# Layer norm, attention and a mixture of experts on one core: experts by chunk, a regrouping done by DMA, and crossed score matmuls

## The reference, cut to what matters

```python
def attn(x, Wq, Wk, Wv):               # x is the layer norm of the input, 4 x 1024 x 256
    Q = (x @ Wq.T).reshape(H, b, s, dkh)          # H = 16 heads, dkh = 16
    K = (x @ Wk.T).reshape(H, b, s, dkh)
    V = (x @ Wv.T).reshape(H, b, s, dvh)
    scores = jnp.einsum('hbqd,hbkd->hbqk', Q, K)
    atten = jax.nn.softmax(scores, axis=-1)
    out = jnp.einsum('hbqk,hbkd->hbqd', atten, V).reshape(b, s, -1)
    y = out + x
    ...                                           # normalised over tokens and features of a batch
def ffn(x, w_gate, w_in, w_out):       # E = 8 experts, two of them weighted per token
    ...
    for e in range(E):
        h = xt @ w_in[e].T
        y = y + gates[:, e:e + 1] * (h @ w_out[e].T)
x = x + attn(xn, ...) + ffn(xn, ...)
```

## Time and profile before

| | us |
|---|---|
| median of 3 runs (lowest to highest) | 1100.63 (1099.38 to 1101.2) |
| the execution that was profiled | 1102.04 |
| its span (first to last instruction) | 1100.2 |

### The profile page before, as it was taken

How to read it: one execution, slowest core, us unless ns; L and a number is a source line. 1 busy time by engine, 2 the same in 40 slices (tenths; PEclk the granted TensorE clock), 3 DMA queues, 4 the chain that set the end, 5 groups by cost and what they waited for, 6 DMA issues and landing times.

```text
span 1100.2 us, 21325 instructions
## 1 busy us (share of the span) xinstructions
PE 999.7 (91%) x7816; PEld 512.7 (47%) x7816; DVE 846.7 (77%) x1108; ACT 648.6 (59%) x1240; POOL 117.2 (11%) x221
## 2 busy tenths in 40 slices
PE   7999999999920699999999999999999999999995
PEld 6888878888710433333333333333333333333332
DVE  5333376767830479999999999999999999999976
ACT  3334310000000048888888888888888888888885
POOL 3221121011111100000000000000000000000001
PEclk9999999999965769999999999999999999999998
DMA  7999697679766512222223232322223232323214
GB/s 269 377 327 330 243 172 187 184 184 227 165 156 154 206 28 54 72 57 70 68 60 72 54 72 54 72 56 71 63 65 72 54 72 54 72 54 72 64 22 154
DMA packets 115766, 133.59 MB, mean 121 GB/s; under 512 B 47328, under 2 KB 84960, under 8 KB 115680
## 3 DMA queue, kind: packets, MB, share of 16 engines
q1 hardware_dynamic: 62560, 77.64, 27.2%
q10 hardware_dynamic: 53120, 54.80, 17.5%
HBM read 80.75 MB, written 50.59 MB: 119 GB/s over the span
## 4 chain that ended last, share of the span: by engine, by line
PE 69%; ACTq 9%; DMA 8%; ACT 5%; issue 5%; POOL 2%; DVE 1%; SPq 0%; POOLq 0%; DVEq 0%
PE ps L959 23%; PE ps L948 21%; PE ps L936 10%; DMA feat_d<-wp 8%; ACTq L529 5%; PE ps L871 4%; PE ps L849 4%; ACTq L518 4%; ACT wp L557 3%; PE ps L860 2%; PE ps L907 2%; PE ps L970 2%; ACT vstage L557 1%; PE ps L982 1%; POOL xnc L396 1%
## 5 line engine op out<-in xcount | busy, mean ns | idle before, releaser
L725 DVE TENSOR_REDUCE negm<-ps 128x1 f32<-128x1024 f32 x512 | 618.7, 1223 | 49.5 <-PE ps L936 40.7
L557 ACT ACTIVATE wp<-ps 128x512 f32<-128x512 f32 x684 | 374.0, 597 | 86.1 <-PE ps L948 62.6
L948 PE MATMUL ps<-qf,xth 50*128 50x512 f32 x1024 | 258.5, 499 | 23.3 <-ACT wp L557 13.8
L959 PE MATMUL ps<-wp,vb 128*17 128x256 f32 x2736 | 216.1, 388 | 0.1
L936 PE MATMUL ps<-xth,qf 48*128 48x512 f32 x1024 | 210.4, 403 | 0.3 <-DVE negm L725 0.3
L948 PEld LDWEIGHTS ps<-qf,xth 50*128 50x128 f32 x1024 | 98.3, 185 | 230.7 <-ACT wp L557 128.3
L557 ACT ACTIVATE vstage<-ps 128x512 f32<-128x512 f32 x170 | 101.7, 598 | 29.4 <-PE ps L948 17.8
L907 PE MATMUL ps<-mth,xtth 128*128 128x512 f32 x256 | 103.7, 405 | 1.0 <-ACT vstage L481 1.0
L936 PEld LDWEIGHTS ps<-xth,qf 48*128 48x128 f32 x1024 | 100.6, 190 | 8.5 <-issue 5.9
L959 PEld LDWEIGHTS ps<-wp,vb 128*17 128x17 f32 x2736 | 46.9, 95 | 118.6 <-ACT wp L557 46.1
L907 PE MATMUL ps<-mtl,xtth 128*128 128x512 f32 x256 | 101.8, 398 | 0.0
(11 more groups left out here) (107 smaller groups left out, 775.8 us busy)
## 6 DMA issues: line engine op xcount, KB each, us to landing
qf<-feat_d SPq DMA_DIRECT2D x128, 192.0 KB, 3.4
feat_d<-wp ACTq DMA_DIRECT2D x32, 512.0 KB
xth<-feat_d SPq DMA_DIRECT2D x128, 96.0 KB, 3.4
wp<-w_in SPq DMA_DIRECT2D x16, 512.0 KB, 5.3
wp<-w_out_t SPq DMA_DIRECT2D x16, 512.0 KB, 6.3
qk_d<-stage ACTq DMA_DIRECT2D x8, 1024.0 KB, 5.1
v_d<-vstage ACTq DMA_DIRECT2D x8, 544.0 KB, 3.2
vb<-v_d SPq DMA_DIRECT2D x128, 34.0 KB, 2.1
```

The source lines that it names most:

```text
L557: nc.scalar.activation(weight_tile(n, j, b)[:, h * HALF:(h + 1) * HALF], ps[:, ST_BANK[(2 * unit + b) % 3], :], ACT.Exp).then_inc(exp_done, 1)
L725: nc.vector.tensor_reduce(negm[:, n % 2, qt:qt + 1], ps[:, b:b + 2, :].rearrange("p b c -> p (b c)"), AX.X, ALU.max, negate=True).then_inc ...
L948: nc.tensor.matmul(ps[:, ST_BANK[(2 * unit + half) % 3], :], kf[rows, u, j * P:(j + 1) * P], qf[rows, u, h * HALF:(h + 1) * HALF], start=T ...
L959: last = nc.tensor.matmul(ps[32 * c:32 * c + VW, PV_BANK, 0:POS // 4], vb[:, n % 2, j + b * NKT // 2, :], weight_tile(n, j, b)[:, c * (POS ...
```

## The change

It does four things.

1. **Order of experts and projections.** All eight expert matrices come first, with the projections of chunk 0 alone between them. The projections of chunk c + 1 are put between the four token tiles of chunk c in stage 2: transposes after tile 0, V after tile 1, Q and K after tiles 2 and 3. The token halves stay in SBUF (`xth`, `xtl`, two chunks deep), so `xth_d` and `xtl_d` and their loads and stores are gone. Projections share PSUM banks 2 and 3. Gates are chosen chunk by chunk on DVE (`choose_experts`, `gate_weights`), where before they were made for all tiles at once. The weights' second half waits for `m_ready`, where it waited for `ml_done`.
2. **Halves before storing, regrouping by DMA.** ACT rounds Q and K while copying them out of PSUM, DVE subtracts for the low half from PSUM (`qk_lo_halves`), and both are stored to `qk_d`, eight DMAs a chunk on ACT's queue. SP then moves `qk_d` to `feat_d` within DRAM, one DMA a block, 64 in all (`regroup`). Each has 64 rows of 16 pieces of 64 numbers (256 bytes). ACT's and POOL's part of the regrouping is gone.
3. **Feature loads.** `feat_d` holds the high and the low half once. A block is loaded with eight DMAs where there were four; the two that fill two copies of the queries' high half read a source whose outermost dimension is a broadcast of 2. Blocks 0 to 3 are loaded after chunk 0's regrouping. `kf` is a tensor of its own. The last chunk's four token tiles (before: the last eight tiles) are mixed with the maxima of blocks 0 and 1, one bank to each maximum.
4. **Crossed products.** In a unit PE does lower scores, upper maxima, lower maxima, upper scores. The lower scores wait for one exponential less than before (`2 * unit - 2`), the upper ones for the same as before.

```diff
+            def regroup(c):
+
+                for half in range(2):
+                    sp.wait_ge(qk_stored[half], 64 * (c + 1))
+                for n in range(BC * c, BC * (c + 1)):
+                    sp.dma_start(feat_d[n].rearrange("f h d (g t) -> (f h d) g t", t=TB),
+                                 qk_d[:, :, :, :, n * TB:(n + 1) * TB].rearrange("g f h d t -> (f h d) g t")
+                                 ).then_inc(regrouped[c], 16)
...
+            regroup(0)
             sp.wait_ge(att_const, 2)
...
+            sp.wait_ge(regrouped[0], 16 * BC)
+            for n in range(SLOTS):
+                features(n)
+            sp.wait_ge(v_stored, 16)
+            values(0)
+            for c in range(1, NC):
+                regroup(c)
             sp.wait_ge(v_stored, 16 * NC)
-            values(0)
             max_rows(0)
...
-                yield qf, slice(first, first + FR), slice(0, POS), feat_d[0, n]
-                yield kf, slice(first, first + FR), slice(0, HALF), feat_d[1, n, :, half * HALF:(half + 1) * HALF]
+                keys = slice(half * HALF, (half + 1) * HALF)
+                yield (qf, slice(first, first + 2 * DH), slice(0, POS),
+                       feat_d[n, 0, 0].unsqueeze(0).to_broadcast([2, DH, POS]))
+                yield qf, slice(first + 2 * DH, first + FR), slice(0, POS), feat_d[n, 0, 1]
+                yield kf, slice(first, first + 2 * DH), slice(0, HALF), feat_d[n, 1, :, :, keys]
+                yield kf, slice(first + 2 * DH, first + FR), slice(0, HALF), feat_d[n, 1, 0, :, keys]
...
             def qk_out(c):
+                act.wait_ge(qk_stored[0], 64 * c)
                 for o in range(4):
+                    act.wait_ge(project_ready, 2 * TC * c + TC + o + 1)
+                    nc.scalar.copy(stage[:, o, :].bitcast(FP32R), ps[:, PROJECT_BANK[o % 2], :]).then_inc(qk_hi, 1)
+                    for half, (done, staged) in enumerate(((qk_hi, stage), (qk_lo, lo_stage))):
+                        act.wait_ge(done, 4 * c + o + 1)
+                        act.dma_start(qk_d[o % 2 * G // 2:(o % 2 + 1) * G // 2, o // 2, half, :, c * CH:(c + 1) * CH],
+                                      staged[:, o, :]).then_inc(qk_stored[half], 16)
...
+            for c in range(NC - 1):
+                for i in range(TC):
+                    add_experts(TC * c + i, range(E // 2))
+                    if i == 0:
+                        lo_halves(c + 1)
+                    elif i == 1 and c + 2 < NC:
+                        layernorm(c + 2)
+                    elif i == 2:
+                        choose_experts(c + 1)
+                        qk_lo_halves(c + 1, range(2))
+                    elif i == 3:
+                        qk_lo_halves(c + 1, range(2, 4))
+                        gate_weights(c + 1)
...
+            for c in range(NC - 1):
+                for i in range(TC):
                     for j in range(E // 2):
-                        y_bank(XS * k + slot, slot, j)
+                        y_bank(TC * c + i, j)
+                    if i == 0:
+                        transposes(c + 1)
+                    elif i == 1:
+                        for t in range(TC):
+                            project_v(c + 1, t)
+                    else:
+                        for o in range(2 * i - 4, 2 * i - 2):
+                            project_qk(c + 1, o)
...
+            def crossed_scores(n, j, h):
+                scores(n, j, h, 0)
+                if n + 2 < NB:
+                    max_scores(n + 2, 2 * j + h, (1,))
+                    max_scores(n + 2, 2 * j + h, (0,))
+                scores(n, j, h, 1)
...
-                        scores(n, j, h)
-                        if n + 2 < NB:
-                            max_scores(n + 2, 2 * j + h)
+                        crossed_scores(n, j, h)
```

More of the change, by code:

```diff
@@ L414, in residual @@
                                         att[:], ALU.add).then_inc(y_done, 1)
[L416 to L417 removed]
+            pool.wait_ge(xn_saved, NC)
             max_halves(0)
@@ L465, in qk_out, with second_weight @@
+            def second_weight(c):
+                act.wait_ge(gap_done, c + 1)
+                rows = slice(TC * c, TC * (c + 1))
+                nc.scalar.activation(ex[:, rows], gap[:, rows], ACT.Exp).then_inc(gexp_done, 1)
             def qk_out(c):
-                act.wait_ge(stage_out, 16 * c)
+                act.wait_ge(qk_stored[0], 64 * c)
                 for o in range(4):
-                    act.wait_ge(qk_ready, 4 * c + o + 1)
-                    nc.scalar.copy(stage[:, o, :], ps[:, QK_BANK[o], :]).then_inc(qk_evac, 1)
@@ L551, in exps @@
+            xt_out(0)
+            m_out(0)
+            v_out(0)
+            second_weight(0)
+            m_out(1)
+            qk_out(0)
+            for e in range(2, E):
+                m_out(e)
+            for c in range(1, NC):
+                xt_out(c)
+                v_out(c)
+                second_weight(c)
+                qk_out(c)
             def exps(n, j, h, b):
@@ L676, in pick, with choose_experts @@
                 g(nc.vector.tensor_tensor(onehot[:, rows], eq[:, rows], wide(first[:, rows]), ALU.is_equal))
-            for chunks, rows in ((NC - 1, slice(0, NT - TC)), (NC, slice(NT - TC, NT))):
-                for h in range(2):
-                    dve.wait_ge(lg_evac[h], 2 * chunks)
+            def choose_experts(c):
+                rows = slice(TC * c, TC * (c + 1))
+                dve.wait_ge(v_evac, 2 * TC * (c + 1))
                 pick(rows, lg, top1, oh1)
@@ L937, in max_scores, with scores @@
                                             kf[rows, u, :], start=True, stop=True)
-                last.then_inc(turn_ready, 1)
-            def scores(n, j, h):
+                if halves != (1,):
+                    last.then_inc(turn_ready, 1)
+            def scores(n, j, h, half):
                 u, unit = n % SLOTS, NKT * n + 2 * j + h
```

448 lines of the change are left out of this document (162 added, 286 removed).

## The result

| | before | after |
|---|---|---|
| median us (lowest to highest) | 1100.51 (1099.38 to 1101.2), 4 runs | 1054.65 (1052.78 to 1056.23), 4 runs |
| the profiled execution, its span | 1102.04, 1100.2 | 1055.4, 1053.6 |

The account below looks back on a forecast made before the run. PE bound the kernel, but for a 57 us regrouping hole and level PE, DVE and exponential loops in stage 3. First scores 344 + stage 3 687.5 + end 15.7 = 1047 span, median 1048; range 1022 to 1090.

Parts of the forecast that it names:

- The hole of 57 us goes: Before stage 3: PE's 56.7 us wait for POOL goes, some 10 return as uncovered weight fetching; first scores 47 earlier.
- The rival that makes it slow: Regrouping: slow DRAM-to-DRAM pieces queue chunks up on SP, first scores wait, 1056 to 1173 us; chance 0.09.
- turning point of 45 us: Regrouping time per chunk at which the change turns slower than before, with first scores 52 later.
- 35 + 8r: Moment in us when the last regrouping ends, if each chunk's takes r us and chunks queue up on SP.
- Stage 1: the step that failed: Expert products: weight-buffer cycle taken as 9 us, five experts 45 us; stage 2 starts at 87, ends 75 and 93.
- Stage 2: A chunk takes 31.7 us on PE, seven 222; DVE needs 29.7, so PE leads; first part ends at 309.
- The rival in which DVE and ACT bound stage 2: Stage 2: DVE and ACT waits raise a chunk to 34 to 36 us, time 1075; chance 0.17.
- Last chunk: End of stage 2: sixteen steps of one bank and one maximum, bound by DVE, 34 us; first scores at 343 to 344.
- Crossing: Stage 3 units: reordered scores and maxima, between 20 us gained and 26 lost, 6 gained taken, giving 687.5.
- cost of split pairs: Stage 3 units: separate waits make a late partner start late; nothing to 0.05 us a unit, 0 to 26 us.
- gain at the write-outs: Stage 3: 0.33 us of PE work pulled out of the stall once a block, 20 us at most.
- Hidden, with about 3 us to spare: Stage 3 feature loads: two broadcast loads on two engines, 53 GB/s, 8 us with latency, hidden; rival of late features 0.07.

Follow-up runs that it names:

- after again: The changed kernel itself, unaltered, profiled once more on another chip as reference for the runs there: 1054.39 us, ratio 0.9563 to the kernel before.
- the kernel with plain loads: Each of the two broadcast feature loads made two plain loads of 16 rows, against the changed kernel: 1050.54 us, ratio 0.9526 to the kernel before.

## Why the prediction was right and where it was wrong

**The hole of 57 us goes.** Right. No idle time of PE from 100 to 800 us is over 3 us, and the regrouping was finished some 20 us before the first scores. That a chunk's regrouping would take at most 18 us was right: 11.1 to 13.8 in after. The rival that makes it slow was real as a mechanism and a good way off: with four times the copies it came, at 53 to 69 us a chunk. Its turning point of 45 us was set too high, though. I let the regrouping start at 35 us, but on SP's queue it stands behind all loads of weights, and chunk 0's first copy went out at 88.38. With 88 + 8r in place of 35 + 8r the same 395 us are reached at r = 38. (The condition written beside that formula, r under 32, should have been r under 40; the time given for r = 36 is right.)

**Stage 1: the step that failed.** The cycle of a weight buffer was taken as 9 us, five times; measured are 12.5, 12.0, 10.4, 9.3 and 10.9. The form of it (half a product, then the refill) was right, both terms were too small. By SP's issues and PE's starts they were:

| cycle | 1 | 2 | 3 | 4 | 5 | sum | taken |
|---|---|---|---|---|---|---|---|
| half a product, until the next issue | 3.6 | 6.6 | 5.4 | 3.7 | 3.7 | 23.1 | 17 (3.4 each) |
| refill, until PE goes on | 8.9 | 5.4 | 5.0 | 5.5 | 7.2 | 32.0 | 28 (5.6 each) |

So the refill, on average 6.4, was within what the row I read gave (6.8) but over the 5.6 that were left in a cycle of 9. The first one is the slow one (9.8 in after again). Chunk 0's eight stores of Q and K, issued from 30.35 to 38.2 us, are the likely reason, since I had only taken out the stores of chunks 1 to 7; no run takes them out, and why the fifth took 7.2 is open. The larger part is the half product of 6.6 us (47.54 to 54.14, when the next issue goes out) and of 5.4: during the wait of 5.4 us the granted clock fell to the lower level, which a row of the trace before already showed for a PE that waits, and a second stretch at 0.50 (60.2 to 63.6 us) slowed the next product. A slow product frees its buffer late, so the next refill is late too. The five distances are 55.1 us where 45 was said, and the last product took 8.8 where I had 6.7: 12.2 us. The rest, 1.3, is at the start: the first V product comes at 17.91 where I took 17.3, and V and Q and K took 0.6 longer together. At the end 0.4 was overestimated, and 86.8 had been rounded to 87, which leaves the 12.9 us. At 99.9 the start of stage 2 is also outside the ends that I gave (75 and 93). In the other kernels with two half buffers it is 96.1 to 98.4, so 1.5 to 3.8 of the 12.9 us belong to this execution. The four-buffer run takes the cause away: on one chip the start of stage 2 falls from 96.1 to 86.0 and the time by 13.6 us.

**Stage 2.** 32.4 us a chunk where 31.7 was said: right within 2%, but seven of them make 4.9 us. A tile takes 5.60 to 5.68 us and not 5.5, the rate of one window (88 products in 20 us), and the projections 9.8 and not 9.6. DVE was said to be busy 0.9 of a chunk and is 0.76 (24.7 us of 32.4). Its sum of 29.7 was too high: the additions of a tile take 3.6 us where nothing holds them up (118.49 to 122.12), not 4.1, which is 2 us a chunk, and the 18 gate instructions about 3.9 us, near 0.22 from start to start, where I had 5. The rest of the 5 us is in layer norm and low halves. The rival in which DVE and ACT bound stage 2 did not come: DVE and ACT do wait for each other there (24.0 us of DVE's subtractions for ACT's copies, in 21 waits), but beside PE's work.

**Last chunk.** 34 to 35 said, 35.0 measured, with DVE at 32.6 of it: right.

**Crossing: the other step that failed, the other way.** I set 6 us, net of 20 gained at the write-outs and of an unknown cost of split pairs, and stage 3 became 17.6 shorter. The cost of split pairs is the term that failed: a lower scores product and an upper maxima product, each with its own wait, start within 0.01 us of each other (717.22 and 717.23), so there is no skew to pay, and common units stayed at 1.22. The gain at the write-outs was right in place: units 4 and 5 fell from 3.48 to 3.26 and 12 and 13 from 2.90 to 2.65, which makes the 0.47 us per 16 units, or 14.5 us over 31 pairs of blocks; what units 7 and 15 gave (0.09 together), unit 6 and others gave back. Of the 0.38 that the write-out unit lost, 0.14 to 0.16 came back in the unit behind it. The other 3 us of the 17.6 are not the crossing: stage 3 of before opened with 20.3 us at the lower clock, that of after with 13.5 (last section). The ceiling of 20 us held against the kernel before; inside the changed kernel the crossing is worth 20.6, since there it also keeps the first units of a block short.

**Feature loads.** "Hidden, with about 3 us to spare" was right for the features and wrong for what stands behind them on the queue. Maxima for a block never waited for a load, but the rows of maxima came up to 0.8 us late in 20 blocks, 9.0 us of waits. Whatever they cost is within what these runs can tell. The prediction held such lateness unlikely because the two engines would be nearly free by the time that the rows are issued; the trace has them at work until then (the window at 602.20). The Trainium skill ("DMA: Bandwidth & Descriptors", section "Rules for kernel authors") says that a leading broadcast of c copies keeps the whole DMA on at most c engines. With c = 2 the trace agrees: a share of 0.13 is 2.1 of sixteen engines, and with the same bytes in loads without an outer dimension of two, and two more issues, the wait disappears. The estimate of 53 GB/s for them was near (49).

**As a whole.** 1054.65 is in the range, 6.6 above the forecast, and 6.1 of it is the sum of +17.8 and -11.7; the rest is the end of stage 3 and rounding. Being near was partly luck.

## What to carry to other kernels

When a load is refilled into the buffer that a product has just left, the cycle is product plus refill, and both ends move: the first refill took 8.9 us where later ones took 5.0 to 7.2, and after the wait of 5.4 us PE came back at the lower clock and freed the next buffer later. Two more half buffers, here in memory that is idle at that stage, saved 13.6 us. In a queue that runs in order, put the work whose inputs are ready ahead of the work that waits for the slow neighbour; splitting a wait without changing the order gave 10.1 us of stage 3, changing the order without splitting 15.6, both together 20.6. And to find out how far a hidden transfer is from being seen, double it and double it again.

## What the runs showed of the hardware that I had not expected

**DRAM to DRAM in small pieces is not slow.** With nothing else running, 32768 pieces of 256 bytes took 36 us, at a share of 1.02 and 232 GB/s (the window above): 16 x 36 / 32768 = 17.6 ns of an engine for a piece. The loads of such pieces into SBUF in the kernel before took 16 x 9 x 1.01 / 4141 = 35 ns each.

**Stage 3 opens at the lower clock, for 10 to 31 us.** In the last chunk PE works 8.3 of 10 us, waiting for DVE; from the start of stage 3 the granted clock is then near 0.5, which is the 1.2 GHz level. How long that lasts differs. Windows of PE (busy, clock, DMA share, GB/s), first of the kernel with plain loads, then of the one with twice the regrouping:

```profile
350.00:360.00 10.00, 8.28 (x36) 1.00 0.01 2
360.00:370.00 10.00, 10.00 (x46) 0.50 0.01 2
370.00:380.00 10.00, 10.00 (x101) 0.99 0.26 69
```

```profile
350.00:360.00 10.00, 8.27 (x36) 1.00 0.15 32
360.00:370.00 10.00, 9.69 (x48) 0.57 0.01 2
370.00:380.00 10.00, 10.00 (x60) 0.50 0.21 60
380.00:390.00 10.00, 10.00 (x59) 0.50 0.04 9
390.00:400.00 10.00, 10.00 (x85) 0.90 0.25 69
```

Their units are equally long later (16 in 21.10 and 21.12), but stage 3 is 674.3 in the one and 683.9 in the other. The count of products in a window shows the price: 59 and 60 at 0.50, 101 at 0.99. The kernel with two copies has runs from 1049.8 us (mean clock 0.985) to 1060.1 (0.977), so its executions may differ in the same way; only the longest was profiled. The kernel before has such a stretch too, and a longer one than after (columns as in rows 2):

```profile
391.30:411.60 20.30, 19.49 (x101) 6.41 (x99) 13.53 (x13) 11.92 (x22) 0.80 (x4) 0.50 0.12 31
```

```profile
364.10:377.60 13.50, 13.46 (x68) 4.60 (x68) 8.94 (x9) 7.90 (x15) 0.41 (x2) 0.50 0.06 14
```

At 59 products in place of 101 in 10 us, the 6.8 us between them are worth an estimated 3 us of stage 3. What decides the length of the low stretch was not tried, and it stays open; nor was it tried to fill the last chunk's waits of PE.
